# A mixture of 32 experts whose blocks of 128 slots become two half blocks of 64, each with weights of its own

## The reference, cut to what matters

```python
logits = x_flat @ router_w.T + router_b
routed_idx = jnp.argmax(logits, axis=-1)

def expert_mlp(w1, b1, w2, b2):          # w1: 256 x 64, w2: 64 x 256
    h = jax.nn.relu(x_flat @ w1 + b1)
    return jax.nn.relu(h @ w2 + b2)
```

## Time and profile before

| | us |
|---|---|
| median of three runs | 3766.42 |
| the profiled execution's own time | 3768.24 |
| its span, first to last instruction | 3766.3 |
| TensorE busy | 3211.5 (85%) |
| VectorE, ScalarE, GpSimd busy | 2513.4, 2065.8, 1935.6 |
| the "sw" section: norm, logits, routing | about 3541 to 3602 |
| its pass loop | 3602 to 3741 |
| its gathering back, and the output | 3741 to 3766 |

### The profile page before, as it was taken

How to read it: one execution, slowest core, us unless ns; L and a number is a source line. 1 busy time by engine, 2 the same in 40 slices (tenths; PEclk the granted TensorE clock), 3 DMA queues, 4 the chain that set the end, 5 groups by cost and what they waited for, 6 DMA issues and landing times. The chain is left out here.

```text
span 3766.3 us, 60909 instructions
## 1 busy us (share of the span) xinstructions
PE 3211.5 (85%) x19844; PEld 2404.9 (64%) x19844; DVE 2513.4 (67%) x3795; ACT 2065.8 (55%) x4488; POOL 1935.6 (51%) x1702
## 2 busy tenths in 40 slices
PE   0959989989986888988888888888988789999767
PEld 0649976668974666666666666666765565666534
DVE  6341136643126999999999999999999644666531
ACT  0332225551227777877777777877776434666511
POOL 0023312101317888889888889898888400000054
PEclk9879989999987999999999999999999998999955
DMA  3039820014951111111111111111111000000045
GB/s 103 2 143 334 323 92 2 2 42 147 333 180 34 46 35 36 46 35 36 46 48 35 49 35 35 47 35 35 46 35 34 23 15 1 2 2 2 18 129 153
DMA packets 133788, 262.81 MB, mean 70 GB/s; under 512 B 14000, under 2 KB 104360, under 8 KB 122952
## 3 DMA queue, kind: packets, MB, share of 16 engines
q1 hardware_dynamic: 122120, 227.64, 18.3%
q0 software_dynamic: 11328, 30.95, 2.5%
HBM read 232.03 MB, written 26.51 MB: 69 GB/s over the span
## 5 line engine op out<-in xcount | busy, mean ns | idle before, releaser
L2013 POOL TENSOR_TENSOR ssm_hc<-ssm_hs,ssm_cb 128x1024 f32<-128x1024 f32 x512 | 1205.2, 2358 | 177.8 <-PE ssm_py L2127 157.8
L2513 DVE TENSOR_TENSOR_SCAN ssm_hs<-ssm_da,ssm_pb 128x512 f32<-128x512 f32 x1024 | 1220.2, 1206 | 97.1 <-POOL ssm_hc L2013 92.4
L2127 PE MATMUL ssm_py<-ssm_hc,ident 128*128 128x256 f32 x4096 | 1071.1, 384 | 40.3 <-POOL ssm_hc L2013 40.3
L2326 ACT ACTIVATE ssm_da<-ssm_dt,ssm_an 128x255 f32<-128x255 f32 x2048 | 863.2, 498 | 191.5 <-DVE ssm_hs L2513 152.4
L2127 PEld LDWEIGHTS ssm_py<-ssm_hc,ident 128*128 128x128 f32 x4096 | 711.4, 192 | 121.1 <-POOL ssm_hc L2013 48.3
L2494 DVE TENSOR_TENSOR ssm_pb<-ssm_pb,ssm_dtu 128x512 f32<-128x512 f32 x832 | 562.7, 676 | 48.3 <-PE ssm_pb L2114 23.8
L2114 PE MATMUL ssm_pb<-ssm_bst,ssm_eyeb 96*128 96x256 bf16 x1664 | 329.1, 280 | 137.3 <-DVE ssm_hs L2513 115.7
L2114 PEld LDWEIGHTS ssm_pb<-ssm_bst,ssm_eyeb 96*128 96x128 bf16 x1664 | 133.8, 99 | 342.7 <-DVE ssm_hs L2513 239.3
L3339 DVE TENSOR_TENSOR moe_hid<-moe_pu,moe_actg 128x512 f32<-128x512 f32 x71 | 49.1, 691 | 349.0 <-PE moe_pu L2982 349.0
L2982 PEld LDWEIGHTS moe_pu<-moe_xt,moe_up 128*128 128x128 f32 x2272 | 267.0, 193 | 6.4 <-ACT moe_xt L3102 3.0
L2982 PE MATMUL moe_pu<-moe_xt,moe_up 128*128 128x128 f32 x2272 | 268.0, 277 | 1.8 <-ACT moe_xt L3102 1.8
(11 more groups left out here) (591 smaller groups left out, 5279.1 us busy)
## 6 DMA issues: line engine op xcount, KB each, us to landing
moe_up<-in_moe_up SPq DMA_DIRECT2D x72, 1024.0 KB, 5.4
ssm_cb<-ssm_c_dram SPq DMA_DIRECT2D x64, 1024.0 KB, 5.6
moe_down<-in_moe_down SPq DMA_DIRECT2D x72, 512.0 KB, 6.2
sw_wt<-in_sw_w SPq DMA_DIRECT2D x47, 192.5 KB
moe_x_dram<-moe_tok SPq DMA_DIRECT2D x32, 128.0 KB
moe_yg<-moe_y_dram SPq DMA_DIRECT2D x16, 256.0 KB, 3.4
tok_w<-in_wd SPq DMA_DIRECT2D x4, 576.0 KB, 13.0
out<-h SPq DMA_DIRECT2D x1, 2056.0 KB, 6.3
```

The lines of the kernel that those rows point to most:

```text
L2013: nc.gpsimd.tensor_tensor(hc[:, n % 2, part_], hs[:, n % 2, part_], cb[:, q % 2, part_, :], ALU.mult).then_inc(s["hc_done"], 1)
L2127: ins = nc.tensor.matmul(sums(j), k.ident[:], hc[:, n % 2, st, :], start=False, stop=(q == QN - 1 and st == NQ_ - 1 and j % 2 == 1))
L2326: ins = nc.scalar.activation(da[:, n % 2, 2 * m + o, 1:L], dt2[:, v, j, 1:L], ACT.Exp, scale=a_n[:, d, j, st:st + 1])
L2513: nc.vector.tensor_tensor_scan(two(hs[:, n % 2, 2 * m:2 * m + 2, :]), two(da[:, n % 2, 2 * m:2 * m + 2, :]), two(pb[:, p % 4]), 0.0, ALU.m ...
```

## The change

For the 32 small experts a pass keeps its 128 slots but now serves two half blocks of PER = 64 slots, each owned by an expert of its own. Experts are padded to 64 slots: NEB = (2056 + 32 x 63) // 64 = 63 half blocks, rounded up to 64, so NBLK = 32 passes. Weights are fetched for each half block, 64 times, into 12 buffers; fetch e waits for pass (e - 12) // 2. In a pass, TensorE widens the columns of each half with its own weights, ScalarE applies each half's bias, and narrow makes two matmuls, whose results go to output rows 0 to 63 and 64 to 127. The gather, the turn, the copy out and the scatter stay one for 128 slots. The routing compares with 33 multiples of 64 in place of 17 of 128 and finds owners for 64 half blocks in place of 47 blocks. For the two gated mixtures HALF is 1, and all values are as before. The diff, without declarations of the buffers that only change NCK to NCB or NBLK to NEB in a shape:

```diff
-    NBLK = (K * NTOK + E * (P - 1)) // P
+    HALF = 1 if glu else 2
+    PER = P // HALF
+    NEB = (K * NTOK + E * (PER - 1)) // PER
+    NBLK = -(-NEB // HALF)
+    NEB = NBLK * HALF
+    NCB = -(-NTOK // PER)
...
-    WR, XR, YR, GR = (4, 4, 3, 6) if glu else (6, 6, 4, 6)
+    WR, XR, YR, GR = (4, 4, 3, 6) if glu else (12, 6, 4, 6)
...
                     if b >= WR:
-                        sp.wait_ge(s["up_done"] if glu else s["y_ps"], (2 if glu else 1) * (b - WR + 1))
+                        sp.wait_ge(s["up_done"] if glu else s["y_ps"], 2 * (b - WR + 1) if glu else (b - WR) // HALF + 1)
...
-                for b in range(NBLK):
+                for b in range(NEB):
                     load_weights(b)
...
                 def widen(b, g):
                     if g or not glu:
                         pe.wait_ge(s["xt_in"], b + 1)
-                        pe.wait_ge(wsem[b % WR], (32 if glu else 16) * (b // WR + 1))
+                        if glu:
+                            pe.wait_ge(wsem[b % WR], 32 * (b // WR + 1))
                         if b >= 2:
                             pe.wait_ge(s["hid_in"], b - 1)
...
                     else:
-                        for c in range(C):
-                            ins = nc.tensor.matmul(pu[0:64, b % 2, 0, 0:P], wt[:, b % WR, c * 64:c * 64 + 64], xt[:, b % 2, c, :], start=(c == 0), stop=(c == C - 1))
+                        for e in range(HALF * b, HALF * b + HALF):
+                            pe.wait_ge(wsem[e % WR], 16 * (e // WR + 1))
+                            at = slice(e % HALF * PER, e % HALF * PER + PER)
+                            for c in range(C):
+                                ins = nc.tensor.matmul(pu[0:64, b % 2, 0, at], wt[:, e % WR, c * 64:c * 64 + 64], xt[:, b % 2, c, at], start=(c == 0), stop=(c == C - 1))
...
                     else:
-                        ins = nc.tensor.matmul(pl[:, 1, 0:D], ht[:, b % 2, :], wt[0:65, b % WR, 128:128 + D], start=True, stop=True)
+                        for e in range(HALF * b, HALF * b + HALF):
+                            at = slice(e % HALF * PER, e % HALF * PER + PER)
+                            ins = nc.tensor.matmul(pl[at, 1, 0:D], ht[:, b % 2, at], wt[0:65, e % WR, 128:128 + D], start=True, stop=True)
                     ins.then_inc(s["y_ps"], 1)
...
-                        nc.scalar.activation(ht[0:64, b % 2, :], pu[0:64, b % 2, 0, 0:P], ACT.Relu, bias=wt[0:64, b % WR, 128 + D:129 + D]).then_inc(s["hid_in"], 1)
+                        for e in range(HALF * b, HALF * b + HALF):
+                            at = slice(e % HALF * PER, e % HALF * PER + PER)
+                            ins = nc.scalar.activation(ht[0:64, b % 2, at], pu[0:64, b % 2, 0, at], ACT.Relu, bias=wt[0:64, e % WR, 128 + D:129 + D])
+                        ins.then_inc(s["hid_in"], 1)
...
-                link(nc.vector.tensor_scalar(k128[:], iota[:, 0:NCK], float(P), None, ALU.mult))
+                link(nc.vector.tensor_scalar(k128[:], iota[:, 0:NCB], float(PER), None, ALU.mult))
...
-                    link(nc.vector.tensor_tensor(cmp_[:], inc[:, :, NCK - 1:NCK].broadcast_to([P, E, NCK]), k128[:].unsqueeze(1).broadcast_to([P, E, NCK]), ALU.is_gt))
+                    link(nc.vector.tensor_tensor(cmp_[:], inc[:, :, NCK - 1:NCK].broadcast_to([P, E, NCB]), k128[:].unsqueeze(1).broadcast_to([P, E, NCB]), ALU.is_gt))
...
-                    link(nc.vector.tensor_tensor(ebc[:], iota[0:1, 0:NBLK].unsqueeze(2).broadcast_to([1, NBLK, E]), binc[0:1, :].unsqueeze(1).broadcast_to([1, NBLK, E]), ALU.is_ge))
+                    link(nc.vector.tensor_tensor(ebc[:], iota[0:1, 0:NEB].unsqueeze(2).broadcast_to([1, NEB, E]), binc[0:1, :].unsqueeze(1).broadcast_to([1, NEB, E]), ALU.is_ge))
...
-                    link(nc.vector.scalar_tensor_tensor(out=pos[:], in0=nb[:].unsqueeze(2).broadcast_to([P, E, NCK]), scalar=float(P), in1=pos[:], op0=ALU.mult, op1=ALU.add))
+                    link(nc.vector.scalar_tensor_tensor(out=pos[:], in0=nb[:].unsqueeze(2).broadcast_to([P, E, NCK]), scalar=float(PER), in1=pos[:], op0=ALU.mult, op1=ALU.add))
```

More of the change, by code:

```diff
@@ L2721, in section_sparse @@
         iota = sb("iota", [P, P])
-        iorev, k128 = sb("iorev", [P, E]), sb("k128", [P, NCK])
+        iorev, k128 = sb("iorev", [P, E]), sb("k128", [P, NCB])
         tri_f, tri = sb("trif", [P, P]), sb("tri", [P, P], BF16)
@@ L2737, in section_sparse @@
         inc, pos = sb("inc", [P, E, NCK]), sb("pos", [P, E, NCK])
-        cmp_ = sb("cmp", [P, E, NCK])
+        cmp_ = sb("cmp", [P, E, NCB])
         nb, binc = sb("nb", [P, E]), sb("binc", [P, E])
         slot_f = sb("slotf", [P, K, NCK])
-        ebc = sb("ebc", [1, NBLK, E])
-        eb_f, eb = sb("ebf", [1, NBLK]), sb("eb", [1, NBLK], mybir.dt.int32)
+        ebc = sb("ebc", [1, NEB, E])
+        eb_f, eb = sb("ebf", [1, NEB]), sb("eb", [1, NEB], mybir.dt.int32)
         rw = sb("rw", [P, C, E + P])
```

## The result

The changed kernel takes **3731.88 us**, the median of 7 runs (3718.47 to 3747.41), against 3770.4 for the kernel before (7 runs, 3755.68 to 3791.05): a ratio of 0.9908, 95% interval 0.9883 to 0.9934. The forecast was 3732 in a range of 3716 to 3753. The profiled execution of after has an own time of 3738.08 and a span of 3736.3.

The account below looks back on a forecast made before the run. The third mixture's loop was taken as bound by TensorE at 1.2 GHz, 2.52 us a pass plus pauses, with GpSimd nearly as full. Loop gain 36.0 less routing 1.5 gave 34.5 us off, hence 3732 us, range 3716 to 3753.

Parts of the forecast that it names:

- The loop before: Third mixture's pass loop in the old kernel: 135.5 us from first transpose to last narrow, 2.88 a pass over 47 passes.
- Widen, 0.85 + 2 x 0.20 = 1.25: TensorE's widen for two experts a pass: 0.85 us streaming plus 0.20 per group behind a wait, 1.25 instead of 1.05.
- weight load of 64 columns: In widen: a load costs about 0.105 us, just hidden under 0.107 us of streaming 64 columns.
- The pauses at a constant share: Loop pauses keep their share because TensorE stays fullest: 2.72 x 2.88 / 2.52 = 3.11 us a pass, 99.5 in all.
- Routing +1.5 us: Path to the first gather: comparison, sum and block steps +2.2 us, three block marks -0.7, net +1.5.
- Narrow's halves side by side: TensorE's narrow: two 64-column matmuls run at once, 0.85 us a pass, not 1.70 one after the other.
- a charge against this edit: Narrow between full-width transposes and half-width matmuls may drain TensorE: at most 0.20 us a pass, 6 us over 32 passes.
- Serial halves: Rival, chance 0.10: narrow's halves run one after the other, 3.57 us a pass, 4.08 with pauses, 3763 us.
- SyncE or DMA as the pace: Rival, chance 0.15: weight fetches at 1.9 us each bound the loop at 117.5 us, 3750 us.
- slower: Rival, chance 0.05: each weight fetch costs 2.6 us at SyncE's issue, loop 153.9 us, 3786 us.
- Faster still: Rival, chance 0.18: pauses belong to GpSimd and go once TensorE is slower, loop 87 us, 3719 us.

Follow-up runs that it names:

- e3: Changed kernel with both halves of narrow writing to the same output rows and ScalarE copying in two pieces: loop 17.0 us more, kernel 3741.11 us.
- e1: Changed kernel with only the first 12 of 64 weight fetches, so no fetch in the loop: loop 93.3 us, kernel 3724.09 us.
- e2: Changed kernel with GpSimd gathering only the first 6 passes' rows; scatters and weight fetches stay: loop 79.4 us, kernel 3707.99 us.
- e8: Changed kernel with experts padded to 32 slots: quarter blocks, 24 passes, 96 fetches, 20 weight buffers; loop 106.0 us, kernel 3734.56 us.
- e12: Changed kernel with plain result stores from ScalarE's queue, results gathered at the end instead of scattered, 20 weight buffers: loop 80.1 us, kernel 3726.85 us.
- e5: Changed kernel with 32 result buffers and all scatters issued after the last gather: loop 105.6 us, kernel 3749.48 us.
- e9: e2 plus one gather a pass from pass 6 on, into tiles nobody reads: loop 98.7 us, kernel 3754.58 us.
- e10: e2 plus a 128x384 addition on GpSimd in place of each dropped gather: loop 74.9 us, kernel 3718.88 us.

## Why the prediction was right

Right in its time and in what makes it: fifteen passes fewer, at nearly the old cost of a pass. That it fits to 0.1 us is luck. The gain was more than forecast, 40.7 us in the section and 38.5 between the medians against 34.5, and the kernel before had a median of 3770.4 over seven runs and not the 3766.42 of the first three; the two errors of 4 us cancel. In the loop it was 42.2 against 36.0: 1.7 by the loop before and 4.5 by that after (99.5 forecast, 95.0 measured). Term by term:

- **The loop before.** I ended it with the narrow at 3739.56 in the chain; one more narrow follows at 3741.27, and its copy starts at 3742.50. 137.2, not 135.5 us: +1.7.
- **Widen, 0.85 + 2 x 0.20 = 1.25.** The mis-sized step, and its reason was wrong. I took the 0.20 for the price of a group that starts behind a wait, and charged it twice. The lines above show that it comes with a change in the number of weight columns. Widen and narrow now both have 64, so widen behind narrow is 0.85, and narrow behind the turn is 1.05 where I had 0.85. The second expert's wait for its weights, long met, costs nothing. 2.52 a pass, not 2.72: 6.4 us, 7.3 with the pauses' share. And no weight load of 64 columns lay open.
- **The pauses at a constant share.** 2.97 / 2.52 = 1.18, where 1.14 was taken (2.88 / 2.52; by the corrected loop it is 2.92 / 2.52 = 1.16). They come to 0.45 us a pass, before to 0.40; the larger share took back 2.9 us (2.52 x 0.036 x 32). Keeping them was right; the reason, that TensorE stays the fullest engine, was not. With widen at 2.72 GpSimd's 2.57 would have had slack; at 2.52 it is the slower of the two, as it was before.
- **Routing +1.5 us.** Comparison and sum +0.54 each, block steps +0.57 each; the three block marks -0.62 together (from the first to the step behind them 1.67 us for 2.29), and VectorE's wait for the inversion on TensorE, which I had left out, 1.63 for 2.29: -0.66. From the opening product to the first gather it is 25.13 before and 26.00 after, **+0.9**. Another 1.0 lies between the first gather and the first turn, 4.05 us for 3.07; in the other runs with halves it is 3.1 to 4.0, so this is no cost of the change that one could name.

Narrow's halves side by side, so that the second costs nothing: right, shown by e3. The Trainium skill, "TensorEngine Tiling (Array Packing)", Key Properties, has a change of tiling mode drain the engine. The traces agree, if 64 and 128 columns of weights count as two modes: about 0.20 us at each change between them. I had it as a charge against this edit, but the kernel before changes as often, twice a pass, only elsewhere, and so the pass stays at 2.52. On weight loads, the Trainium skill, "TensorE: Matmul & The Clock Gate", Part 3 (they overlap running matmuls only when the row group differs), stays contradicted: widen's eight records with eight loads take 0.85 us, what their streaming of 8 x 64 columns takes by the same count that gave 0.85 for narrow in the earlier trace rows.

The rivals. *Serial halves* would have been 3.37 a pass, as e3 shows, not 3.57. *SyncE or DMA as the pace* and *slower*: both rested on issue times seen in the loop (1.4 and 2.6 us). e1 and e2 show that those were the pace of freed buffers and pauses, not a price; e8 shows the price, 1.1 us. The rival becomes true at quarters. *Faster still* had the right suspect for the pauses, and e3 bears out its condition, a TensorE slower than GpSimd. It did not come about, as far as the sums tell, because TensorE turned out 0.20 faster than I had charged: 2.52 against GpSimd's 2.57. No run has TensorE at 2.72. With hardly a pause the loop takes 79 to 80 us (e2, e12).

## What to carry to other kernels

Count passes, not their contents: where a pass of small matmuls carries fixed instructions for a full tile, packing two half tiles with different weights into it costs nothing as long as outputs lie in different rows and the issuing queue keeps up. When groups of small matmuls alternate, count how often the number of weight columns changes from one to the next, at 0.20 us each here. Take an issue time seen inside a loop as a price only where nothing held the queue back. And before a loop is tuned for TensorE, see what GpSimd does beside it: two indirect transfers a pass, one every 1.27 us, unbroken, cost more than their own time.

## What was not expected of the hardware

- While GpSimd issues indirect transfers 1.27 us apart without a break, the messages by which TensorE releases ScalarE and VectorE come late: ScalarE is idle for 2.1 to 3.7 us at a time in the middle of after's loop, and for 7.3 and 9.3 us in e5, VectorE there for 15.0. Most of the long pauses of after and e9 end 0.9 to 1.3 us behind the last issue of the stretch. That is no rule: the one of the earlier trace rows ends 0.13 us behind it (3661.01 against 3660.88), and several in e5 end in the middle of a stretch. Additions on GpSimd of about the same length don't do it (e10 against e9), nor does one indirect transfer a pass once the loop runs (e12). How the two are coupled inside the chip was not tried and stays open; so does which step is held: the end of TensorE's matmul (which the profile models), its signal, or the signal's arrival.
- A group of matmuls whose number of weight columns differs from that of the group ahead (128 and 64 here) takes 0.20 us longer at 1.2 GHz. By the lines of e5 below it is about 0.15 for turn and narrow at 2.4 GHz (an estimate: 0.37 and 0.58 against half of 0.43 and 0.85).
- Two matmuls with 64 columns of weights each, over 256 columns, into different halves of the output rows, run beside each other: 1.05 against 1.90 us.
- TensorE is at 1.2 GHz in all of after's loop, but e5 has a stretch from 3640 to 3660 at a mean of 0.93, behind passes that ran without pauses; at 2.4 GHz a pass is 0.58 + 0.46 + 0.37 = 1.41 us there:

```profile
3641.35 0.58 PE ln_ps L3008 x4
3641.93 0.46 PE sw_pu L2995 x8
3642.39 0.37 PE sw_pz L2976 x2
```

  From 3653 on SyncE's issues at 1.1 us each end that pace. A loop freed of its pauses meets the weights next.
